# Attention scores per head on 32-row tiles of TensorE in plain fp32, in place of three fp32r passes over block-diagonal keys

## What is computed

```python
def _L0_xattn_ref(q, k, v, Wq, bq, Wk, bk, Wv, bv, Wo, bo):
    qh = (q @ Wq.T + bq).reshape(B, Nq, H, D).transpose(0, 2, 1, 3)      # H = 16, D = 32
    kh = (k @ Wk.T + bk).reshape(B, Nkv, H, D).transpose(0, 2, 1, 3)     # Nkv = 77
    vh = (v @ Wv.T + bv).reshape(B, Nkv, H, D).transpose(0, 2, 1, 3)
    attn = jax.nn.softmax(jnp.einsum('bhqd,bhkd->bhqk', qh, kh) * D ** (-0.5), axis=-1)
    out = jnp.einsum('bhqk,bhkd->bhqd', attn, vh)
    return out.transpose(0, 2, 1, 3).reshape(B, Nq, C) @ Wo.T + bo

x = x + tanh(g_xattn[0]) * _L0_xattn_ref(_layernorm(x), ctx, ctx, ...)
x = x + tanh(g_ffn[0]) * _L0_ffn_ref(_layernorm(x), ...)   # router (512 x 8), top 2 of 8 experts, 2 shared
x = x + tanh(g_xattn[1]) * _L1_xattn_ref(_layernorm(x), ctx)
x = x + tanh(g_ffn[1]) * _L1_ffn_ref(_layernorm(x), ...)
```

## Time and profile before

| | us |
|---|---|
| median of three executions | 2009.84 |
| the profiled execution, its own time | 2011.05 |
| its span, first to last instruction | 2009.5 |
| first scores of step 0 in it | 78.70 |
| first scores of step 1 | 101.22 |
| first scores of step 15 | 508.02 |
| end of the attention stage, about | 561 |

### The profile page before, as it was taken

The page is one execution under the profiler, slowest core; times in us unless marked ns, Lnnn a source line. Parts: engine busy times, 40 slices in busy tenths (PEclk is TensorE's granted clock), DMA queues, the critical chain, the costliest instruction groups (busy, mean ns, idle before and its releaser), DMA issues. The chain is left out here.

```text
span 2009.5 us, 26103 instructions
## 1 busy us (share of the span) xinstructions
PE 1665.4 (83%) x8557; PEld 1291.8 (64%) x8572; DVE 1272.0 (63%) x2058; ACT 717.7 (36%) x1289; POOL 594.6 (30%) x544
## 2 busy tenths in 40 slices
PE   7599989999759999989999995676487877887776
PEld 5587878778648888877788883444265545554452
DVE  3588788888463455422333332788569889888986
ACT  2244344344224222223334441455454323433330
POOL 0132323332224454644110002544004214431442
PEclk9799899998769999999999997566588988898888
DMA  3112221221189889734433335867320111111011
GB/s 118 43 58 69 84 78 57 73 84 64 48 303 313 292 317 325 285 112 160 136 110 105 106 108 172 297 227 261 110 82 1 62 52 54 45 40 70 14 42 42
DMA packets 108197, 252.02 MB, mean 125 GB/s; under 512 B 15027, under 2 KB 15027, under 8 KB 103912
## 3 DMA queue, kind: packets, MB, share of 16 engines
q1 hardware_dynamic: 65272, 121.98, 17.9%
q0 software_dynamic: 17056, 67.12, 9.3%
q10 hardware_dynamic: 25808, 62.14, 8.7%
HBM read 147.13 MB, written 101.97 MB: 124 GB/s over the span
## 5 line engine op out<-in xcount | busy, mean ns | idle before, releaser
L1274 PE MATMUL e_u_ps<-e_w,e_xeT 128*128 128x512 f32 x1596 | 395.0, 400 | 10.7 <-DVE e_xeT L1179 10.7
L1274 PEld LDWEIGHTS e_u_ps<-e_w,e_xeT 128*128 128x128 f32 x1596 | 294.1, 189 | 74.4 <-DVE e_w L1228 8.8
L1813 POOL TENSOR_TENSOR b_h<-b_h,b_srow 128x512 f32<-128x512 f32 x120 | 162.4, 1393 | 385.4 <-ACT b_srow L1839 385.4
L1950 PE MATMUL b_f_ps<-b_xdT,w1q 128*128 128x512 f32 x1024 | 258.0, 407 | 15.4 <-DVE b_av L1886 9.6
L1950 PEld LDWEIGHTS b_f_ps<-b_xdT,w1q 128*128 128x128 f32 x1024 | 194.0, 192 | 68.2 <-DVE b_av L1886 15.7
L1285 PE MATMUL e_y_ps<-e_w,e_hT 128*128 128x512 f32 x798 | 210.5, 406 | 4.4 <-DVE e_hT L1210 2.9
L1925 PE MATMUL b_o_ps<-w2q,b_hq 128*128 128x512 bf16 x434 | 122.7, 446 | 60.9 <-DVE b_x L1855 35.0
L1285 PEld LDWEIGHTS e_y_ps<-e_w,e_hT 128*128 128x128 f32 x798 | 143.6, 190 | 31.3 <-issue 4.0
L1831 ACT ACTIVATE b_av<-b_f_ps,cb,cw 128x512 f32<-128x512 f32 x128 | 98.9, 773 | 163.3 <-PE b_f_ps L1950 162.7
L1925 PEld LDWEIGHTS b_o_ps<-w2q,b_hq 128*128 128x128 bf16 x448 | 48.7, 113 | 132.4 <-DVE b_x L1855 38.1
L1824 ACT ACTIVATE b_h<-b_av 128x512 f32<-128x512 f32 x128 | 80.2, 626 | 137.0 <-DVE b_av L1886 136.8
(11 more groups left out here) (207 smaller groups left out, 2825.4 us busy)
## 6 DMA issues: line engine op xcount, KB each, us to landing
e_xe<-slots_in_scratch SPq DMA_DIRECT2D x69, 256.0 KB
experts_out_scratch<-e_ye ACTq DMA_DIRECT2D x69, 256.0 KB, 2.0
xin<-in_x SPq DMA_DIRECT2D x16, 512.0 KB, 3.8
xres<-in_x SPq DMA_DIRECT2D x16, 512.0 KB, 4.5
x_scratch<-x SPq DMA_DIRECT2D x32, 256.0 KB, 2.1
xn_scratch<-xn SPq DMA_DIRECT2D x32, 256.0 KB, 2.1
e_xe<-xn_scratch SPq DMA_DIRECT2D x32, 256.0 KB
e_fraw<-in_w1T ACTq DMA_DIRECT2D x8, 1024.0 KB
```

The costliest lines, as they stand in the source:

```text
L1274: mm = pe.matmul(u_ps[:, i], xeT[:, pa, k], w[:, par, pb, k * 2 * HID:(k + 1) * 2 * HID], start=(k == 0 and (pa, pb) == PASSES[0]), stop=( ...
L1813: pool.tensor_tensor(h[:, 1 - par, m], h[:, 1 - par, m], srow[:], ALU.mult).then_inc(u_done, 1)
L1950: mm = pe.matmul(f_ps[:, m % RING], w1q[:, k, m * P:(m + 1) * P], xdT[:, part, k], start=(k == 0 and part == 0), stop=(k == KD - 1 and par ...
```

## The change

Scores are now one plain fp32 product per head: `qT` of that head is 32 rows by 128 columns, `kc` 32 rows by 77 columns. Head i of each group stands on partitions 32i to 32i+31, so four consecutive matmuls use four different 32-row tiles of TensorE; they write to four different banks, `s_ps[:, i]`, at column g x 77. There are 16 matmuls per half, then one `s_full`; the first matmul of a half waits until both pairs of the half before have been read (`s_sub`). VectorE's softmax instructions keep their number and sizes, with the heads in another order, which `pT` undoes. Queries are kept whole in fp32: ScalarE writes `qT` out of PSUM and raises `q_done`, VectorE's L634 and the split keys (L483, L546), the copy `vb` (L506) and the clearing of `kbd` are gone. `m_free` no longer counts queries, and `room` tells which semaphore frees a bank of `m_ps`. `whole` writes out all 18 calls in place of the loop.

```diff
         def whole(eng, run):
 
-            run(-1, -1, False, False, True)
-            run(0, 0, True, False, True)
-            run(1, 0, True, True, True)
-            if B > 2:
-                with eng.Fori(1, B - 1) as b:
-                    run(b * 2, b, True, True, True, 0)
-                    run(b * 2 + 1, b, True, True, True, 1)
-            run(NSTEP - 2, B - 1, True, True, True)
-            run(NSTEP - 1, B - 1, True, True, False)
-            run(NSTEP, B, False, True, False)
+            for s in range(-1, NSTEP + 1):
+                run(s, s // 2, 0 <= s < NSTEP, s >= 1, s < NSTEP - 1)
...
+        def room(s, u, mid, back, front):
+
+            d, q, i = before(s, 0, 0, 6), before(s, 0, 2, 0), int(u[1])
+            if u[0] == "o":
+                if isinstance(s, int) and s == 1:
+                    return q_done, q - 1 + i
+                return m_free, d - 1 + i
+            if u[0] == "w":
+                return m_free, d + 1 + i
+            if u[0] == "q":
+                if back:
+                    return m_free, d + 3 + i
+                return (q_done, q - 1 + i) if s >= 0 else None
+            return (q_done, q + 1 + i) if front else (m_free, d + 3 + i)
...
                         for g in range(2):
-                            act.activation(qT[:, 1 - par, 0, 2 * i + g], m_ps[:, m[u] % 2, g * W2:(g + 1) * W2],
-                                           ACT.Identity, bias=bq_s[:, 2 * i + g:2 * i + g + 1]).then_inc(m_hi, 1)
+                            ins = act.activation(qT[:, 1 - par, 2 * i + g], m_ps[:, m[u] % 2, g * W2:(g + 1) * W2],
+                                                 ACT.Identity, bias=bq_s[:, 2 * i + g:2 * i + g + 1])
+                        ins.then_inc(q_done, 1)
...
                 def softmax_in(j):
                     for pair in range(2):
-                        dve.wait_ge(s_full, s * 4 + 2 * j + pair + 1)
+                        dve.wait_ge(s_full, s * 2 + j + 1)
...
-                if par == 1 and front:
-                    keys(b + 1)
...
                 def scores(j):
+                    use = s * 2 + j
+                    if use:
+                        pe.wait_ge(s_sub, use * 2)
                     for g in range(NG):
-                        if g % 2 == 0 and not (isinstance(s, int) and s * 4 + 2 * j + g // 2 < 2):
-                            pe.wait_ge(s_sub, s * 4 + 2 * j + g // 2 - 1)
-                        for pa, pb in PASSES:
-                            mm = pe.matmul(s_ps[:, g, 0:GC], qT[:, par, pa, g, j * P:(j + 1) * P], kbd[:, pb, g, :],
-                                           start=((pa, pb) == PASSES[0]), stop=((pa, pb) == PASSES[-1]))
-                        if g % 2:
-                            mm.then_inc(s_full, 1)
+                        for i in range(HG):
+                            rows = slice(i * HD, (i + 1) * HD)
+                            mm = pe.matmul(s_ps[:, i, g * C:(g + 1) * C], qT[rows, par, g, j * P:(j + 1) * P],
+                                           kc[rows, b, g, :], start=True, stop=True)
+                    mm.then_inc(s_full, 1)
...
                 if mid:
 
-                    if par == 0:
-                        pe.wait_ge(k_bd, b * HG + HG)
-                    pe.wait_ge(m_free, mb)
+                    pe.wait_ge(q_done, before(s, 0, 2, 0))
                     scores(0)
```

More of the change, by code:

```diff
@@ L307, in attention @@
         xT = sb("xT", [P, 2, KD, W2], FR)
-        qT = sb("qT", [P, 2, 2, NG, W2], FR)
+        qT = sb("qT", [P, 2, NG, W2], F32)
         prob = sb("prob", [P, 2, H, C], F32)
@@ L420, in run @@
                     for j in range(2):
-                        sp.wait_ge(m_free, m_base(s) + plan(mid, back, front)[1][f"w{j}"] + 1)
+                        sp.wait_ge(m_free, before(s, 0, 0, 6) + 3 + j)
                         sp.dma_start(n.tile_rows(n.x1_d, (s - 1) * 2 + j), x1[:, j]).then_inc(x1_out, 16)
@@ L478, in run @@
                 t, m = plan(mid, back, front)
[L480 to L484, removed]
                 def tcopy(u, dst, done, parts=P):
@@ L511, in run @@
                     exps(1)
-                    for g in range(NG):
-                        tcopy(("p", 0, g), pT[:, g * HG:(g + 1) * HG, 0:P], p_free, C)
-                if par == 1 and front:
-                    keys(b + 1)
+                    for i in range(HG):
+                        tcopy(("p", 0, i), pT[:, i * NG:(i + 1) * NG, 0:P], p_free, C)
                 if front:
@@ L521, in run @@
                         for g in range(2):
-                            act.activation(qT[:, 1 - par, 0, 2 * i + g], m_ps[:, m[u] % 2, g * W2:(g + 1) * W2],
-                                           ACT.Identity, bias=bq_s[:, 2 * i + g:2 * i + g + 1]).then_inc(m_hi, 1)
+                            ins = act.activation(qT[:, 1 - par, 2 * i + g], m_ps[:, m[u] % 2, g * W2:(g + 1) * W2],
+                                                 ACT.Identity, bias=bq_s[:, 2 * i + g:2 * i + g + 1])
+                        ins.then_inc(q_done, 1)
                 if mid:
-                    for g in range(NG):
-                        tcopy(("p", 1, g), pT[:, g * HG:(g + 1) * HG, P:W2], p_free, C)
+                    for i in range(HG):
+                        tcopy(("p", 1, i), pT[:, i * NG:(i + 1) * NG, P:W2], p_free, C)
             whole(act, run)
@@ L535, in run @@
                 t, m = plan(mid, back, front)
-                hb = before(s, 0, 4, 2)
+                hb = before(s, 0, 0, 2)
+                db = before(s, 0, 0, 6)
                 sb0 = before(s, 0, 2, 2)
[L541 to L548, removed]
                 def xlow(j):
@@ L628, in run @@
                                           ALU.mult).then_inc(xn2_done, 1)
[L629 to L643, removed]
                 if back:
+                    for j in range(2):
+                        dve.wait_ge(t_full, tb + t[f"n{j}"] + 1)
+                        dve.tensor_copy(x2T[:, :, j * P:(j + 1) * P],
+                                        t_ps[:, t[f"n{j}"] % 2].rearrange("p (a b) -> p a b", b=P)).then_inc(n_free, 1)
                     for j in range(2):
@@ L671, in m_room @@
                 def m_room(u):
-                    if not (isinstance(s, int) and mb + m[u] < 2):
-                        pe.wait_ge(m_free, mb + m[u] - 1)
+                    need = room(s, u, mid, back, front)
+                    if need is not None:
+                        pe.wait_ge(*need)
                 def scores(j):
+                    use = s * 2 + j
+                    if use:
+                        pe.wait_ge(s_sub, use * 2)
                     for g in range(NG):
-                        if g % 2 == 0 and not (isinstance(s, int) and s * 4 + 2 * j + g // 2 < 2):
-                            pe.wait_ge(s_sub, s * 4 + 2 * j + g // 2 - 1)
-                        for pa, pb in PASSES:
-                            mm = pe.matmul(s_ps[:, g, 0:GC], qT[:, par, pa, g, j * P:(j + 1) * P], kbd[:, pb, g, :],
-                                           start=((pa, pb) == PASSES[0]), stop=((pa, pb) == PASSES[-1]))
-                        if g % 2:
-                            mm.then_inc(s_full, 1)
+                        for i in range(HG):
+                            rows = slice(i * HD, (i + 1) * HD)
+                            mm = pe.matmul(s_ps[:, i, g * C:(g + 1) * C], qT[rows, par, g, j * P:(j + 1) * P],
+                                           kc[rows, b, g, :], start=True, stop=True)
+                    mm.then_inc(s_full, 1)
                 def prob_transposes(j):
@@ L702, in run @@
                     pe.wait_ge(p_free, s * 2 * NG)
-                    pe.wait_ge(v_done, b if par == 0 else b + 1)
                     for i in range(2):
@@ L723, in run @@
                 if back:
-                    pe.wait_ge(m_free, mb + m["o1"] + 1)
+                    pe.wait_ge(m_free, before(s, 0, 0, 6) + 2)
                     for j in range(2):
```

26 lines of the change are left out of this document (8 added, 18 removed).

## The result

The changed kernel takes 2024.53 us (median of seven executions, 2021.89 to 2026.28); the kernel before, run beside it, has 2009.84 (seven executions, 2003.07 to 2017.75). The ratio is 1.0076, 95% interval 1.0055 to 1.0097: slower by 0.8%, where 0.8% faster was forecast (1993 against 2009.84). The profiled execution took 2023.87 us.

What follows compares the result with a forecast made beforehand. Steps 1 to 14 were taken as 26.8 us of work each, plus key waits (10.5 us) and lost clock (21.1 us). Terms +3.9 - 10.5 - 0.9 - 10.1 = -17.6 us from 2011.05 gave 1993; range 1976 to 2028.

Steps and rivals of the forecast that it cites:

- Cost of the scores: Scores on TensorE: four row tiles overlap, eight groups at 0.113 us, so 0.90 us per half instead of 1.95.
- What the faster scores bring: nothing: Front of a step: the saved 2 us become idle before scores(1), w starts as before; +0.06 us per step.
- Tile shapes: Two more TensorE shape changes per step, around the scores; with the later hand-over 0.26 x 15 steps = +3.9 us.
- Keys: Tail of seven odd steps: n no longer waits for VectorE's low parts of the next keys; -10.5 us.
- Queries: First step: scores(0) waited 1.93 us for VectorE's query part, now gone, ScalarE's part remains; -0.9 us. Steady steps gain nothing.
- The loop written out: All calls written out: the loop's branch costs TensorE nothing, as step 8 right behind it is shortest; 0.
- Clock: Attention steps: of 21.1 us lost to low granted clock, 11 stay, with one step in two having a low stretch; -10.1 us.
- Rival 3: Clock also falls in the front, w begins at 1.2 GHz every other step, every tail has its low stretch; 2016 us, 11%.

Runs made afterwards that it cites:

- dense_both: Changed kernel plus eight unused dense matmuls behind o and eight between n and r, where TensorE waits: 1979.77 us, ratio 0.9831.
- keys_late: Kernel before with VectorE's key parts moved behind the second pair of query parts, so n does not wait: 1998.47 us, ratio 0.9913.
- dense_whole: Kernel before, dense fp32r scores kept, with scores handed over whole per half, late key parts and the loop written out: 2001.90 us, ratio 0.9929.
- scores_twice: Changed kernel with each tiled scores matmul done twice, same result: 2063.73 us, ratio 1.0241.
- swapped: Changed kernel with scores(0) of a step put ahead of the p(1) transposes of the step before, no added work: 1973.42 us, ratio 0.9789.

## Why the prediction was wrong, step by step

- *Cost of the scores*: right. The source line L649 of the changed kernel, durations in ns min/median/max, has its shortest matmul at 0.27 us (row below). Forecast four loads side by side, 0.113 per group, hand-over after 1.2 us; at full clock 32 matmuls cover 1.13 us and the hand-over comes after 1.19. The eight groups measure (1.13 - 0.27) / 7 = 0.123 us apart at most, 0.98 in all, which is near the 0.90 forecast. The Trainium skill (TensorE: Matmul & The Clock Gate, "Packing small matmuls") has 3.07 for four row tiles of 512 columns. At the 77 columns of this kernel the trace does not bear out the 1.18 us estimated from it.

```profile
L649 PE MATMUL s_ps<-k_all,qT x1024: 270/413/493, 76.7 to 534.9; 32*128 32x77 f32 x171
```

- *"What the faster scores bring: nothing"*: right. Expected scores(1) 4.4 and w 7.0 us after scores(0); dense_both shows 4.42 and 6.98.
- *Tile shapes* and the later hand-over: +0.26 per step forecast; dense_both's 26.76 us in step 2, with filling, is 0.04 below the 26.80 of the earlier trace rows. Zero, within what the rows resolve.
- *Keys*: right; n follows q at once, and keys_late gained 0.9%, of which the 10.5 us are half a percent.
- *Queries*: right; the wait ahead of the first scores fell from 1.93 us to 0.93. They start at 76.74 instead of 78.70, so another microsecond was gained ahead of that wait, which the forecast did not have.
- *The loop written out*: put at nothing. Taken alone it measured 0.3% faster. In the profiled executions the stages behind the attention are 8.1 us shorter with the change, but other kernels that write the loop out differ by 9.8 us in that part, so the cause stays open.
- *Clock*: this step failed. It said "Every step is now like an even one" and "I take one in two, 11 us". Fourteen steps of 26.76 are 374.6 us; they took 428.0, so the clock cost 53.4 us, not 11. Two things are in this. First, one in two was too few even for the old scores: with the wait for the keys gone and dense scores in place (keys_late), nearly every step had its low stretch, 21.4 us in all. Second, what I compared with, step 2, had dense scores behind its tail. The change takes these away. With them gone, the low stretch that begins in p(1) goes on through scores(0), o, scores(1) and x at half speed, and ends in w. That is the other 32 us.

That the form of the work behind the tail matters is shown by dense_whole against scores_twice, and by the fillings. That the dense scores themselves used to bring the clock back is argued. In the kernel before, the low stretch from the tail of step 1 reached 0.8 us into the scores of step 2, but the one of step 7 ended at 305.18, 0.5 us ahead of the scores, while TensorE was at the transposes p(1). The window of that stretch, r and p(1) at half clock from end to end:

```profile
298.35:305.18 6.83, 6.23 (x29) 5.94 (x30) 3.13 (x9) 1.19 (x2) 0.22 (x2) 0.50 0.50 161
```

So transposes did not always leave the clock low, and the runs do not say which of the four blocks of the front is to blame.

The 42 us missed there, less the 8 of the later stages and some 4 of tile shapes and hand-over, are the gap between 1993 and 2024.5. The cost of a low stretch was also taken low: 1.57 us is step 2's, while step 7 lost 31.24 - 26.80 - 1.51 = 2.93 us to its longer one. Rival 3 named this mechanism and its place, with 11%, and priced it at 2016; it took the low stretches of tail and front as separate, 1.57 us and 0.85 us a step, where they joined and cost 3.9 in a step of 30.7. The earlier trace rows showed that the tail can lose the clock, and the change replaced the work behind it; what thin work would do there no row of the kernel before could tell.

## What to carry to other kernels

A saving of TensorE time off the critical path turned into idle here, and idle and thin work cost the clock of what stood behind it: before shrinking matmuls, look at what precedes each low PEclk stretch and ask what now brings the clock back. Price such a change at both clocks, and give the freed time to other work by order (swapped, 2% faster) before taking it as a gain. Here the loss showed in the windows as one low stretch at the same place in nearly every step. And before a few microseconds in an untouched stage are put down to an edit, compare that stage over several kernels that share the edit.

## What was not expected of the hardware

- Four 32-row tiles in plain fp32, each with its own bank, loaded and ran side by side: 32 loads and 32 matmuls in 1.13 us at full clock.
- TensorE was busy for 13.40 of 13.65 us at 1.2 GHz, with transposes, tiled matmuls and the first 2.4 us of dense ones, before the full clock came back. In step 7 of the kernel before it came back after 6.83 us of eight-column matmuls and transposes alone.
- Filling idle places with 2.3 to 2.5 us of unused matmuls a step took the changed kernel from a ratio of 1.0076 to 0.9831 (dense) or 0.9838 (column tiles).
